# Wider gaps between VectorE's questions and ScalarE's answers in the last chunk of a two-layer graph attention kernel, and three sign comparisons moved from VectorE to ScalarE

## The reference

```python
# layer 0: 4 heads of 32
Wh = (h @ W).reshape(N, H, D)
e = s_src[:, None, :] + s_dst[None, :, :]
e = where(e >= 0, e, 0.2 * e); e = where(adj > 0, e, NEG_INF)
h_prime = einsum('ijh,jhd->ihd', softmax(e, axis=1), Wh)
x = layernorm(x + elu(h_prime))
# layer 1: one head of 128, hyperbolic
x_tan = logmap0(x)                 # arctanh(norm) * x / norm
e = leaky_relu(x_tan @ a[:D] + (x_tan @ a[D:]).T, 0.2)
x = layernorm(x + proj(expmap0(softmax(where(adj > 0, e, NEG_INF)) @ x_tan)))
```

## Time and profile before

| | us |
|---|---|
| runs without a profile | 907.83, 908.23, 909.77 |
| the profiled execution | 909.87 |
| its span, first to last instruction | 908.1 |
| busy TensorE (matmuls) | 841.8, 93% |
| busy VectorE | 769.1, 85% |
| busy ScalarE | 682.8, 75% |
| mean granted TensorE clock | 0.978 |

### The profile page before, as it was taken

One profiled execution on the slowest core, in us unless ns is written; L12 is line 12 of the kernel. 1 busy time (PEld: TensorE's weight loads), 2 busy tenths in 40 slices (PEclk: granted clock), 3 DMA queues, 4 the chain that ended last, 5 costly groups with the idle time before them and its releaser, 6 DMA issues.

```text
span 908.1 us, 24394 instructions
## 1 busy us (share of the span) xinstructions
PE 841.8 (93%) x10868; PEld 688.5 (76%) x10868; DVE 769.1 (85%) x1318; ACT 682.8 (75%) x803; POOL 43.3 (5%) x80
## 2 busy tenths in 40 slices
PE   8687999988999889999998999699999999999994
PEld 6686999988999879999998985355555555555552
DVE  3978898899988999889999899785877687878876
ACT  3999898898999989999995776778374554638222
POOL 3200000000000000000000000000000000000000
PEclk9899999999999999999998999799999999999997
DMA  8999377803758226204031002430335353544000
GB/s 147 176 105 248 53 71 94 238 26 31 90 71 177 106 25 80 40 22 191 26 118 25 2 9 86 71 105 13 105 92 172 120 185 113 189 138 141 2 12 14
DMA packets 42065, 84.67 MB, mean 93 GB/s; under 512 B 6242, under 2 KB 31332, under 8 KB 41316
## 3 DMA queue, kind: packets, MB, share of 16 engines
q0 software_dynamic: 12416, 33.56, 26.0%
q1 hardware_dynamic: 29540, 49.50, 15.4%
HBM read 112.27 MB, written 21.12 MB: 147 GB/s over the span
## 4 chain that ended last, share of the span: by engine, by line
PE 49%; ACT 24%; DVE 22%; issue 5%; DMA 0%; SPq 0%; DVEq 0%; ACTq 0%
PE bank L688 22%; PE bank L1299 21%; ACT ring L620 12%; ACT masks L767 7%; DVE ring L633 3%; DVE ring L653 3%; PE bank L1289 2%; PE bank L536 2%; ACT masks L523 2%; ACT moving L573 1%; DVE ring L657 1%; DVE ring L663 1%; DVE evac L704 1%; ACT masks L543 1%; PE bank L1228 1%
## 5 line engine op out<-in xcount | busy, mean ns | idle before, releaser
L688 PE MATMUL bank<-moving,ring 128*128 128x99 bf16 (+1 forms) x6528 | 451.8, 218 | 12.2 <-DVE ring L663 8.8
L688 PEld LDWEIGHTS bank<-moving,ring 128*128 128x128 fp8e4 x6528 | 387.8, 98 | 14.7 <-DVE ring L663 10.0
L620 ACT ACTIVATE ring<-s_rows,scores 128x1024 fp8e4<-128x1024 f32 x360 | 380.9, 1143 | 3.6 <-PE bank L688 2.8
L688 PE MATMUL bank<-moving,masks 128*128 128x99 bf16 x1664 | 221.9, 209 | 16.2 <-DVE evac L704 11.7
L1299 PE MATMUL bank<-moving,masks 128*128 128x387 bf16 x1056 | 178.2, 327 | 0.0
L688 PEld LDWEIGHTS bank<-moving,masks 128*128 128x128 fp8e4 x1664 | 162.9, 98 | 18.2 <-DVE ring L657 8.8
L767 ACT ACTIVATE masks<-s_rows,adj_tiles 128x512 fp8e4<-128x512 f32 x256 | 157.9, 709 | 0.6 <-DVE moving L745 0.5
L1299 PEld LDWEIGHTS bank<-moving,masks 128*128 128x128 fp8e4 x1056 | 101.7, 96 | 73.0
L653 DVE SCALAR_TENSOR_TENSOR ring<-ring,masks 128x1024 int32<-128x1024 int32 x90 | 109.6, 1217 | 8.1 <-ACT ring L620 8.0
L663 DVE TENSOR_TENSOR ring<-masks,ring 128x1024 int32<-128x1024 int32 x76 | 93.1, 1225 | 26.9 <-PE bank L688 25.1
L395 ACT ACTIVATE ring<-ring 128x4 f32<-128x4 f32 (+1 forms) x24 | 4.9, 205 | 136.4 <-DVE ring L311 110.7
(11 more groups left out here) (214 smaller groups left out, 636.9 us busy)
## 6 DMA issues: line engine op xcount, KB each, us to landing
masks_kept<-masks SPq DMA_DIRECT2D x4, 4096.0 KB, 16.8
masks<-masks_kept SPq DMA_DIRECT2D x8, 2048.0 KB, 9.8
adj_tiles<-in_adj_dram POOLq DMA_DIRECT2D x24, 512.0 KB, 8.0
s_rows<-score_rows SPq DMA_DIRECT2D x14, 512.0 KB, 4.9
ring<-masks_kept POOLq DMA_DIRECT2D x11, 512.0 KB, 3.9
first_part<-masks_kept POOLq DMA_DIRECT2D x11, 512.0 KB, 3.9
second_part<-masks_kept POOLq DMA_DIRECT2D x10, 512.0 KB, 3.9
adj_tiles<-in_adj_dram POOLq DMA_DIRECT2D x16, 256.0 KB, 15.4
```

What stands on the lines that cost most here:

```text
L620: last = act.activation(j_tile(below, k), s_rows[:, h % 2, :], ACT.Sign, bias=scores[:, g * JU + k, h:h + 1], saturate=False)
L688: last = pe.matmul(bank[b][:, at + lo:at + hi], mask, moving[:, j, h, lo:hi], start=first, stop=(j == T - 1), skip_group_check=True)
```

## The change

ScalarE makes the signs of units 9, 22 and 30 of the last chunk, which VectorE compared before (25 units against 22, VectorE 7 against 10). The answers and questions are put behind later units:

| step | behind unit, before | after |
|---|---|---|
| ScalarE: Sqrt, Ln, late_exp | 15, 17, 20 | 16, 19, 23 |
| ScalarE: round_part1 (0,0), (0,1), (1,0), (1,1) | 23, 25, 28, 30 | 25, 27, 29, 31 |
| VectorE: roots_ask, logs_ask, gains | 12, 14, 16 | 12, 15, 18 |
| VectorE: late factors / weights | 19 / 19 | 18 / 21 |
| VectorE: weigh_group(0), take_high1(0), take_middle1(0) | 20, 22, 24 | 21, 23, 25 |
| VectorE: weigh_group(1), take_high1(1), take_middle1(1) | 25, 27, 30 | 26, 28, 30 |

```diff
-              "AVAAVAAA" "AVAAVAAA" "AVAAVAVA" "AVAAVAVA"]
+              "AVAAVAAA" "AAAAVAAA" "AVAAVAAA" "AVAAVAAA"]
...
-                            if u == 15:
+                            if u == 16:
                                 act.wait_ge(roots_asked, 1)
...
-                            if u == 17:
+                            if u == 19:
                                 act.wait_ge(logs_asked, 1)
...
-                            if u == 20:
+                            if u == 23:
                                 late_exp(act, 0)
-                            if u == 23:
+                            if u == 25:
                                 round_part1(act, 0, 0)
-                            if u == 25:
+                            if u == 27:
                                 round_part1(act, 0, 1)
-                            if u == 28:
+                            if u == 29:
                                 round_part1(act, 1, 0)
-                            if u == 30:
+                            if u == 31:
                                 round_part1(act, 1, 1)
...
-                def late_weights(n):
+                def late_factors(n):
                     lo, hi = (0, EARLY) if n == 0 else (EARLY, T)
                     dve.wait_ge(scores1_ready, n + 1)
                     dve.tensor_scalar(rows[:, 0, lo:hi], s1[:, lo:hi], 0.0, None, ALU.min)
                     dve.tensor_scalar(rows[:, 1, lo:hi], s1[:, lo:hi], 0.0, None, ALU.max).then_inc(factors_asked, 1)
+
+                def late_weights(n):
+                    lo, hi = (0, EARLY) if n == 0 else (EARLY, T)
                     dve.wait_ge(exp1_given, 4 * n + 2)
...
-                            if u == 14:
+                            if u == 15:
                                 dve.wait_ge(roots_given, 1)
                                 logs_ask(step, rows, inv_std, 0, EARLY, logs_asked)
-                            if u == 16:
+                            if u == 18:
                                 dve.wait_ge(logs_given, 1)
                                 gains(step, rows, inv_std, 0, EARLY, d1, s1, scores1_ready)
-                            if u == 19:
+                                late_factors(0)
+                            if u == 21:
                                 late_weights(0)
-                            if u == 20:
                                 dve.wait_ge(kept, 16 * (NC - 1))
                                 dve.wait_ge(unit_done, (NC - 1) * U)
                                 weigh_group(dve, 0)
-                            if u == 22:
+                            if u == 23:
                                 take_high1(dve, 0)
-                            if u == 24:
+                            if u == 25:
                                 take_middle1(dve, 0)
-                            if u == 25:
+                            if u == 26:
                                 dve.wait_ge(unit_done, (NC - 1) * U + 2 * UH)
                                 weigh_group(dve, 1)
-                            if u == 27:
+                            if u == 28:
                                 take_high1(dve, 1)
```

More of the change, by code:

```diff
@@ L1535, in _ @@
                 gains(step, rows, inv_std, EARLY, T, d1, s1, scores1_ready)
+                late_factors(1)
                 late_weights(1)
```

## The result

Six runs of each on one chip: before 907.59 to 909.77, median 908.74 us; after 911.91 to 915.27, median 912.66 us. The ratio is **1.0045, with a 95% interval of 1.0027 to 1.0063**: 4.1 us slower (2.5 to 5.7). The profiled execution after took 915.27 us, 5.4 more than the profiled one of before, with a span of 913.5 us. Both profiled executions took longer than the median run of their kernel (915.27 is the highest of the six after, 909.87 is above all six of before), so a difference between the two traces is good to about 2 us only.

A forecast was written before the change was run, and what follows sets the result against it. TensorE was taken to set the pace. Its later pause, net +2.95 us, became +2.9 us at split_group(1) and at the end: span 908.1 to 911.0, or 911.1 us against the median of 908.23; range 903.2 to 912.8.

The forecast's parts named there:

- third head: Last chunk's units 16 to 23 on TensorE: 36.2 us before against 29.7 for equal work; unit 23 forecast at 516.1.
- pause: TensorE idle under "issue", no semaphore: moves from unit 18 to mid unit 20, taken as 5 us; net +2.95 us.
- scattered store: Early scores, 12 KB as 3072 pieces of 4 B: issued about 485.8, 10.6 us later, landing 16.9 us after issue.
- the link: TensorE's instruction packet due at 490 is held by the store until 501.1; TensorE runs dry from about 496.
- the ledger up to the store: Time account, last chunk: roots at 468.5, unit 16 at 478.75 (+1.85 us), store issued about 485.8.
- The wait for the roots: VectorE behind unit 15 waits for ScalarE's Sqrt until 468.5: 3.3 us, where it had no wait.
- the wait in front of unit 27: Last head: TensorE through with unit 26 at 527.6, unit 27 ready only at 529.1.
- The two later comparisons on ScalarE: Units 22 and 30 add 8.3 us on ScalarE, covered by its idle 9.92 us; costed at nothing.
- A clock drop at 478.75: Possible slow clock behind the idle time before unit 16, worth 1.7 us; claimed to change nothing, TensorE still resuming at 501.1.
- B: Rival: TensorE's pause stays at unit 18, only the late take_head counts; +1.7 us, 909.9 us; chance 0.15.
- C: Rival: no TensorE pause in the new order; -5.0 us, or -3.3 with a clock drop, 903.2 to 904.9; chance 0.27.
- D: Rival: roots come in time, no 3.3 us wait at unit 15, pause remains; -0.4 us, 907.8 us; chance 0.10.

The follow-up runs named there:

- b_flat: Kernel before, early-score store written as 128 pieces of 96 B instead of 3072 of 4 B (output order wrong, timing only); ratio to before 0.9975.
- a_flat: Changed kernel, early-score store written as 128 pieces of 96 B instead of 3072 of 4 B (output order wrong, timing only); ratio to before 0.9987.
- the turned versions: Kernels in which TensorE transposes the early scores and they are stored as 24 rows of 512 B; b_turned 0.9982 and a16_turned 0.9972 to before.
- b_store18: Kernel before, SyncE waiting for the end of unit 17 before issuing the early-score store in 4 B pieces; ratio to before 1.0028.
- a_table: Changed kernel with the old table of comparisons (VectorE takes units 9, 22, 30 back), new places kept; ratio to before 1.0017.
- best_scatter: Changed kernel, logs_ask behind unit 16, late_exp behind 22, weigh_group(1) behind 27, early store in 3072 pieces of 4 B; ratio to before 1.0012.
- a16_turned: Changed kernel with logs_ask behind unit 16 and early scores transposed on TensorE, stored as 24 rows of 512 B; ratio to before 0.9972.
- a_logs16: Changed kernel with logs_ask behind unit 16 instead of 15, store in 4 B pieces as it was; ratio to before 1.0006.
- b_table: Kernel before with only the new table (ScalarE makes signs of units 9, 22, 30), questions and answers in old places; ratio to before 1.0030.
- b_turned: Kernel before with early scores transposed on TensorE ahead of unit 18 and stored as 24 rows of 512 B; ratio to before 0.9982.

## Why the prediction was right or wrong

**Right: what bounds.** TensorE's third head and its pause were the place, and the scattered store is what makes the pause: b_flat, a_flat and the turned versions take it away with the store's small pieces, and b_store18 moves it with the store.

**Not shown: the link.** The prediction said that an instruction packet is held back by the store and that TensorE runs dry one packet, 7.3 us, after it would have asked for it. That was argued from one trace. What speaks for a link is that in the trace after no packet starts for 12.0 us (484.75 to 496.75), though one was due near 492. But the rule does not fit the times. The packet of 484.75 had moved within 0.9 us, so before the store was issued at 486.35, and TensorE stopped at 492.24 all the same, when the next one was only due and not 7.3 us later. From the start of the last packet in time to the first stop it is 13.5 us before, 7.5 us after, and about 8 in a_table and best_scatter. And in the trace before, the late packet of 484.25 had moved by 486.5, while the longest stop came behind it, from 487.87 to 490.48. Nor is it the room on the DMA engines: in the trace before, their share (last column but one) is high only while the pieces move, and zero in the pause, though the store landed at 492.1:

```profile
476.50:476.75 0.25, 0.00 (x0) 0.00 (x0) 0.25 (x2) 0.00 (x0) 0.00 (x0) 1.00 0.76 7
488.00:488.25 0.25, 0.00 (x0) 0.00 (x0) 0.25 (x1) 0.25 (x1) 0.00 (x0) 1.00 0.00 0
```

So in what way the store stops TensorE stays open; no run separates the instruction packet from another way. The rule in the Trainium skill ("Runtime: NRT & Kernel Launch", section "Instruction fetch mechanics") gives TensorE 128 KiB of instructions in blocks of 16 KiB. As an estimate from this figure, eight blocks of 7.3 us would carry it over a packet that is 5 us late. If the packets are the link, the seven traces with the scattered store speak against such a stock; if they are not, the traces say nothing of it. The same skill's "DMA: Bandwidth & Descriptors", section "Specifications", says that below 512 B the DMA engine misses its line rate and does a read-modify-write. The 96 B pieces are below this too, and landed after 1.4 us where the 4 B pieces took 15.6 for the same 12 KB. So it is the number of pieces, or how small they are, and not the limit alone, that made the difference here.

**Right, nearly to the number: the ledger up to the store.** The wait for the roots was forecast at 3.3 us and measured 3.52; the roots at 468.5, measured 469.0; TensorE's unit 16 at 478.75, measured 479.30 (0.36 us of that is a later start of the chunk, 416.57 against 416.21, from before the change's place); the store at 485.8, measured 486.35. From take_head on the ledger holds as well: 30.3 us to split_group(1), 30.05 forecast, with the wait in front of unit 27 at 1.5 us, measured 1.57. The two later comparisons on ScalarE, put at nothing, made VectorE wait 1.75 us for round_part1, but behind this it waited 5.17 us for TensorE at take_head anyway, so they did cost nothing in the changed kernel.

**Wrong: the third head.** I forecast 2.9 us and measured 4.1 (5.25 in the profiled pair). The step that failed is the sentence that "A clock drop at 478.75 would not change this, since TensorE would still resume at 501.1", by which the clock's 1.7 us entered the sum as nothing. The clock did drop, for 3.4 us (1.7 us of work lost), and the pause did not swallow it. The ledger had TensorE at work until 496, in the middle of unit 20, and idle for 5 us. In the trace it stopped at 492.24, at the end of unit 18, idled 3.8 us in four pieces, and resumed for good at 498.11, 11.8 us behind the store's issue instead of 15.3 (the other six traces give 14.3 to 15.5), with about five microseconds of work less done. Unit 23 ended at 518.2, not 516.1. These 2.1 us are made up of the later start of unit 16 (+0.55), the shorter pause (-1.2) and the time that TensorE was busy beyond its work (5.5 us for the 2.8 that the ledger left room for, +2.7, of which 1.7 is the clock drop that was put at nothing). With the 0.2 of the last head they are nearly the whole difference between the 2.9 forecast and the 5.25 in the trace. Why TensorE stopped so early is not known, as said above. That the forecast is not further off is in part luck: a pause sized 1.2 us too long hid part of the clock drop that was left out.

**The rivals.** B and C are out: without the pause the change would not be slower than before (a_flat 0.9987), but the pause does not stay in unit 18 and did not vanish. For C I forecast 903.2 to 904.9 us. a_flat makes its condition true, with the clock drop, and in its trace the ledger holds: split_group(1) forecast at 540.35 + 1.7 = 542.05, measured 542.21, which is 3.2 us ahead of the trace of before. Yet the runs of a_flat are only 1.1 us faster than before's (907.33 against 908.38 us on the same chip). The ledger carried the distance between two traces over to the medians, and the profiled execution of before (909.87 us) lies 1.1 us above the median of its six runs and 1.6 above that of the three. For a16_turned (901 us expected, 907.16 measured) the ledger itself failed: it followed one engine through the last head and missed the wait in front of unit 27 (2.55 us) and the clock drop behind it, and split_group(1) came at 542.65, not 538. D was nearly right in price: a_logs16 is the change without the wait for the roots, forecast -0.4 us, measured +0.5 (-0.5 to +1.5).

## What to carry to other kernels

Before you give questions more room, count for each answer how many units stand ahead of it on the engine that answers: here one more unit on ScalarE and an answer one unit later put the answer 8.4 us back, while VectorE came to collect it only one unit later. An "issue" pause of TensorE with no semaphore is worth a look at the DMAs in flight: a store of 12 KB in 4 B pieces, for which no engine was waiting at the time, cost 2.3, 3.6 and about 5 us in three schedules. Give a clock drop its own term in the sum, and do not let a later pause swallow it without a reason. And before a ledger that starts from one trace is carried over to a median, see where that execution lies among the runs: here this alone was worth over 1 us.

## What the runs showed of the hardware

- A store of 12 KB from SBUF to DRAM took 15.4 to 16.9 us to land in 3072 pieces of 4 B (before, after and b_store18, the traces that show its landing) and 1.4 us in 128 pieces of 96 B (b_flat, a_flat).
- While the scattered store was under way TensorE stopped under "issue" for 2.3 to 4.4 us, in two to five pieces of 0.15 us and more, and resumed for good 11.8 to 15.5 us behind its issue, in all seven traces that have it; in none of the six without it is there such a pause in that head. In the trace before the DMA engines were idle during the longest of these pieces (share 0.00 at 488.00).
- The clock fell to the 1.2 GHz level, for 3.4 us, at the end of or behind 3.23 us (after), 2.96 us (a_flat), 2.55 us (a16_turned) and 2.29 us (b_turned, in front of unit 24) without matmuls, but not behind 2.97 us (b_table, in front of unit 16) or 2.21 us (b_flat, in front of unit 24). In best_scatter it stayed at 1.00 through the whole third head, although the pauses there make 3.75 us in four pieces; in the trace after, four pieces of 3.77 us in all did bring it down. So the length of the idle time alone does not tell the two apart here, and what does was not tested.
